# Attention scores as three 64-row products in alternating halves of the array, in a fused decoder block

## What is computed

```
q = xn @ Wq.T ; kv = xn @ Wkv.T ; k, v = kv[..., :64], kv[..., 64:]     # 16 heads of q, one k, one v
q, k = l2norm(q), l2norm(k)                                             # then both times sqrt(16)
sim = where(causal_mask, max_neg, einsum('bhid,bjd->bhij', q, k))
out = einsum('bhij,bjd->bhid', softmax(sim), v)
x = x + layernorm(out @ Wout.T, g2)
```

## Time and profile before

| | us |
|---|---|
| median of 3 runs (lowest, highest) | 1096.88 (1095.97, 1097.26) |
| the profiled execution, its time | 1095.58 |
| its span, first to last instruction | 1093.8 |
| TensorE busy (matmuls) | 917.9 |
| VectorE, ScalarE, GpSimd busy | 709.3, 444.0, 228.6 |

### The profile page before, as it was taken

One profiled execution on the slowest core, in us unless ns is written; L12 is line 12 of the kernel. 1 busy time (PEld: TensorE's weight loads), 2 busy tenths in 40 slices (PEclk: granted clock), 3 DMA queues, 4 the chain that ended last, 5 costly groups with the idle time before them and its releaser, 6 DMA issues.

```text
span 1093.8 us, 14277 instructions
## 1 busy us (share of the span) xinstructions
PE 917.9 (84%) x4446; PEld 676.6 (62%) x4446; DVE 709.3 (65%) x1607; ACT 444.0 (41%) x808; POOL 228.6 (21%) x282
## 2 busy tenths in 40 slices
PE   3698998898999987978989898999871089999997
PEld 2466666575766765755766566666551067777775
DVE  4466888868788877668787788877576322222221
ACT  1364643545454544434554445443342112222221
POOL 3232321211211123213122121201010611111111
PEclk8699998989998988989999999989985589999999
DMA  8300000000000000000000000000334500000000
GB/s 270 53 1 1 1 1 1 1 1 1 1 1 1 1 1 1 1 1 1 1 1 1 1 1 1 1 1 1 112 119 153 173 7 25 23 24 29 20 25 4
DMA packets 19176, 29.02 MB, mean 27 GB/s; under 512 B 2080, under 2 KB 15649, under 8 KB 19105
## 3 DMA queue, kind: packets, MB, share of 16 engines
q1 hardware_dynamic: 17008, 22.73, 7.0%
q0 software_dynamic: 1680, 4.21, 1.1%
q10 hardware_dynamic: 416, 1.18, 0.3%
HBM read 21.41 MB, written 7.10 MB: 26 GB/s over the span
## 4 chain that ended last, share of the span: by engine, by line
PE 36%; DVE 10%; issue 5%; POOL 3%; ACT 2%; DMA 1%; DVEq 0%; POOLq 0%; ACTq 0%
PE W L1278 6%; PE S L1255 5%; PE O L1255 5%; PE W L1166 2%; PE O L1095 2%; DVE ph L826 2%; PE O L1092 2%; PE W L1208 2%; PE S L1076 2%; PE S L1077 2%; PE O L1093 2%; POOL sorted_rows L581 2%; DVE junk L948 1%; DVE pl L828 1%; DVE mx L910 1%
## 5 line engine op out<-in xcount | busy, mean ns | idle before, releaser
L617 ACT ACTIVATE pr<-S 128x512 f32<-128x512 f32 x288 | 172.1, 598 | 255.5 <-PE S L1077 252.8
L828 DVE TENSOR_TENSOR pl<-pr,ph 128x512 fp32r<-128x512 f32 x288 | 206.0, 715 | 9.9
L1092 PE MATMUL O<-ph,vhi 128*65 128x512 f32 x288 | 145.6, 506 | 50.9 <-DVE ph L826 50.7
L826 DVE CAST ph<-pr 128x512 fp32r<-128x512 f32 x288 | 122.9, 427 | 54.5 <-POOL pr L535 38.6
L1095 PE MATMUL O<-pl,vhi 128*65 128x512 f32 x288 | 121.7, 423 | 1.7 <-DVE pl L828 0.5
L1076 PE MATMUL S<-qT,kT 128*128 128x512 f32 x288 | 120.1, 417 | 0.0
L1077 PE MATMUL S<-qT,kT 128*128 128x512 f32 x288 | 119.1, 414 | 0.0
L1093 PE MATMUL O<-ph,vlo 128*65 128x512 f32 x288 | 119.0, 413 | 0.0
L1092 PEld LDWEIGHTS O<-ph,vhi 128*65 128x65 f32 x288 | 41.5, 144 | 77.5 <-DVE ph L826 50.7
L528 POOL TENSOR_TENSOR rs<-ri,half 128x1 f32<-128x1 f32 x48 | 31.2, 650 | 238.0 <-DVE ri L762 238.0
L535 POOL TENSOR_SCALAR_AFFINE_SELECT pr<-pr 128x512 f32<-128x512 f32 x64 | 45.5, 711 | 166.3 <-ACT pr L617 166.3
(11 more groups left out here) (169 smaller groups left out, 1643.5 us busy)
## 6 DMA issues: line engine op xcount, KB each, us to landing
raw<-in_w_v SPq DMA_DIRECT2D x16, 512.0 KB, 6.3
wps<-in_w_proj SPq DMA_DIRECT2D x4, 1024.0 KB, 9.3
sorted_rows<-pad_row SPq DMA_DIRECT2D x19, 128.5 KB, 5.0
xs<-sorted_rows SPq DMA_DIRECT2D x19, 128.5 KB, 2.0
wqkv<-in_wqkv_t ACTq DMA_DIRECT2D x1, 1152.0 KB, 6.2
wout<-in_wout_t SPq DMA_DIRECT2D x1, 1024.0 KB, 10.0
xall<-in_x SPq DMA_DIRECT2D x1, 1024.0 KB, 11.0
xall<-in_x SPq DMA_DIRECT2D x1, 768.0 KB, 7.9
```

The source lines that it names most:

```text
L617: nc.scalar.activation(pr[:, k % RING, :], S[k % AHEAD][:], ACT.Exp, scale=SIM_SCALE)\
L826: nc.vector.tensor_copy(ph[:, k % RING, :], pr[:, k % RING, :]).then_inc(ph_ready, 1)
L828: nc.vector.tensor_tensor(pl[:, k % RING, :], pr[:, k % RING, :], ph[:, k % RING, :].bitcast(F32), ALU.subtract).then_inc(pl_ready, 1)
L1092: nc.tensor.matmul(o, vhi[:, vs, 0:DH + 1], ph[:, k % RING, :], start=j == 0, stop=False)
```

## The change

- **Scores.** The parts of q are no longer stacked. `qTh` and `qTl` hold high and low parts of two heads one under the other, 64 rows each. Of eight neighbouring heads the four even ones are now a group with an even number and use rows 0 to 63, the four odd ones are the next group and use rows 64 to 127. Per step there are three products of 64 rows (high by high, key high by q low, key low by q high), and the scores of two steps, (t, g, j) and (t, g + 1, j), are issued together, product by product, alternating between the halves and two banks. The fourth product, low by low, is left out.
- **Order.** Steps go (g, j), (g + 1, j), (g, j + 1) and so on, so O0 and O1 fill at the same time. Scores are issued every second step, for the steps four and five ahead; there are four banks S, two banks W. `LATER` is 3 for VectorE and 4 for ScalarE and GpSimd. Rings are 6 deep. A tile too short for side work gets 8 empty positions first, then its steps.
- **Exponential.** Off the diagonal ScalarE takes it twice from the bank: into `ph` in fp32r, then into `pr`; VectorE's cast stays on the diagonal alone.
- **Turning.** `qn` is turned in full float32, two heads at a time: eight transposes in two jobs, and one for the doubled key. ScalarE copies a job out as the high part, then VectorE subtracts that from the bank for the low part (`q_low`) and so frees the bank. `lows_early` sees that the subtraction stands, in the order, ahead of the job that needs its bank. GpSimd makes the value's parts itself (`v_parts`).
- **Hidden turn** of the feed-forward: banks S2, S3 in place of W2, S2.

The diff, cut to its core:

```diff
-RING = 4
+RING = 6
 KV = TPB + 2
 XS = 4
-WB = 3
+WB = 2
...
-    ("out_turn", 0, -1, 0.10), ("q_high", 0, 1, 0.11), ("out_turn", 1, -1, 0.12), ("q_low", 0, 1, 0.16),
+    ("out_turn", 0, -1, 0.10), ("k_double", 0, 1, 0.08), ("out_turn", 1, -1, 0.12), ("v_parts", 0, 1, 0.16),
...
-AHEAD = 3
-
-
-LATER = {"pe": 0, "dve": 2, "act": 3, "pool": 3}
+AHEAD = 4
+
+
+LATER = {"pe": 0, "dve": 3, "act": 4, "pool": 4}
...
     for t in range(TILES):
-        for g in range(GROUPS):
-            start.append(len(steps))
-            steps += [(t, g, j) for j in range(t % TPB + 1)]
+        start.append(len(steps))
+        for g in range(0, GROUPS, 2):
+            steps += [(t, g + s, j) for j in range(t % TPB + 1) for s in range(2)]
     start.append(len(steps))
     return steps, start
...
+def lows_early(here):
+
+    owed = []
+    for stages in here:
+        n = 0
+        while n < len(stages):
+            name, part, t = stages[n]
+            if name in READER:
+                for entry in owed:
+                    entry[1] += 1
+                for key, _ in [entry for entry in owed if entry[1] >= WB]:
+                    for later in here:
+                        if key in later:
+                            later.remove(key)
+                    n = stages.index((name, part, t))
+                    stages.insert(n, key)
+                    n += 1
+                owed = [entry for entry in owed if entry[1] < WB]
+                if name == "q_turn":
+                    owed.append([("q_low", part, t), 0])
+            elif name == "q_low":
+                owed = [entry for entry in owed if entry[0] != (name, part, t)]
+            n += 1
...
-            own = range(start[GROUPS * slot], start[GROUPS * (slot + 1)])
+            own = range(start[slot], start[slot + 1])
             ks = []
             most = len(own) - AHEAD
             for n, k in enumerate(own[:most]):
-                ks += [k] + [None] * (max(most, MIN_POSITIONS - AHEAD) * (n + 1) // most - len(ks) - 1)
-            ks += own[most:]
+                ks += [k] + [None] * (max(most, MIN_POSITIONS) * (n + 1) // most - len(ks) - 1)
+            if most <= 0:
+                ks = [None] * MIN_POSITIONS
+            ks += own[max(most, 0):]
...
-        HT = [W[2], S[2]]
+        HT = [S[2], S[3]]
...
-                    elif name == "q_low":
-
-                        pool.wait_ge(qhi_ready, t + 1)
-                        pool.wait_ge(qlo_ready, t + 1)
+                    elif name == "v_parts":
+
+                        pool.wait_ge(qn_ready, t + 1)
                         if t >= KV:
-                            pool.wait_ge(pv_done, group_start[GROUPS * TPB * ((t - KV) // TPB + 1)])
+                            pool.wait_ge(pv_done, tile_start[TPB * ((t - KV) // TPB + 1)])
                         vs = t % KV
-                        nc.gpsimd.tensor_copy(vhi[:, vs, 0:DH], qhl[:, HEADS + 1, 0, :].bitcast(F32)).then_inc(v_ready, 1)
-                        nc.gpsimd.tensor_copy(vlo[:, vs, 0:DH], qhl[:, HEADS + 1, 1, :].bitcast(F32)).then_inc(v_ready, 1)
+                        nc.gpsimd.tensor_copy(vhi[:, vs, 0:DH], qn[:, HEADS + 1, :]).then_inc(v_ready, 1)
+                        pool.wait_ge(v_ready, 2 * t + 1)
+                        nc.gpsimd.tensor_tensor(vlo[:, vs, 0:DH], qn[:, HEADS + 1, :], vhi[:, vs, 0:DH].bitcast(F32),
+                                                ALU.subtract).then_inc(v_ready, 1)
...
-                act.wait_ge(pv_done, group_start[G_ + 1])
+                act.wait_ge(pv_done, group_last[G_] + 1)
...
+                    if not on_diagonal(k):
+                        if k >= RING:
+                            act.wait_ge(pv_done, k - RING + 1)
+                        nc.scalar.activation(ph[:, k % RING, :], S[k % AHEAD][:], ACT.Exp, scale=SIM_SCALE)\
+                            .then_inc(ph_by_act, 1)
...
-                    elif name == "q_high":
-                        act.wait_ge(qn_ready, t + 1)
-                        if t >= 1:
-                            act.wait_ge(side_ready, job_count("q_turn", 4, t - 1))
-                            act.wait_ge(v_ready, 2 * t)
-                            act.wait_ge(kdup_ready, 2 * t)
-                        nc.scalar.copy(qhl[:, :, 0, :], qn[:]).then_inc(qhi_ready, 1)
-                    elif name == "q_turn" and part < 4:
+                    elif name == "q_turn" and part < 2:
                         act.wait_ge(side_ready, job + 1)
                         if t >= 2:
-                            act.wait_ge(s_ready, group_start[GROUPS * (t - 1)])
-                        nc.scalar.copy(qT[t % 2][:, 4 * part:4 * part + 4, :].rearrange("p h q -> p (h q)"),
-                                       W[job % WB][:]).then_inc(act_freed, 1)
-                    elif name == "q_turn" and part == 4:
+                            act.wait_ge(s_ready, tile_start[t - 1])
+                        nc.scalar.copy(qTh[t % 2][:, 4 * part:4 * part + 4, :].rearrange("p h q -> p (h q)"),
+                                       W[job % WB][:]).then_inc(qth_ready, 1)
+                    elif name == "q_turn" and part == 2:
                         act.wait_ge(side_ready, job + 1)
                         if t >= KV:
-                            act.wait_ge(s_ready, group_start[GROUPS * TPB * ((t - KV) // TPB + 1)])
-                        nc.scalar.copy(kT[:, t % KV].rearrange("p a k -> p (a k)"), W[job % WB][:, 0:2 * P])\
-                            .then_inc(act_freed, 1)
+                            act.wait_ge(s_ready, tile_start[TPB * ((t - KV) // TPB + 1)])
+                        nc.scalar.copy(kT[:, t % KV, 0, :], W[job % WB][:, 0:P]).then_inc(qth_ready, 1)
...
-                    nc.vector.tensor_copy(ph[:, k % RING, :], pr[:, k % RING, :]).then_inc(ph_ready, 1)
-                    dve.wait_ge(ph_ready, k + 1)
+                    if on_diagonal(k):
+                        nc.vector.tensor_copy(ph[:, k % RING, :], pr[:, k % RING, :]).then_inc(ph_by_dve, 1)
+                    ph_wait(dve, k)
...
+                    elif name == "k_double":
+                        dve.wait_ge(qn_ready, t + 1)
+                        nc.vector.tensor_copy(kdup[:], qn[:, HEADS, :].unsqueeze(1).broadcast_to([P, 2, DH])).then_inc(kdup_ready, 1)
                     elif name == "q_low":
-                        dve.wait_ge(qhi_ready, t + 1)
-                        nc.vector.tensor_tensor(qhl[:, :, 1, :], qn[:], qhl[:, :, 0, :].bitcast(F32), ALU.subtract)\
-                            .then_inc(qlo_ready, 1)
-                        dve.wait_ge(qlo_ready, t + 1)
-                        for n in range(2):
-                            nc.vector.tensor_copy(kdup[:, n], qhl[:, HEADS, n, :].bitcast(F32).unsqueeze(1).broadcast_to([P, 2, DH]))\
-                                .then_inc(kdup_ready, 1)
+                        turn = job_of["q_turn", part, t]
+                        dve.wait_ge(qth_ready, 3 * t + part + 1)
+                        if part < 2:
+                            nc.vector.tensor_tensor(
+                                qTl[t % 2][:, 4 * part:4 * part + 4, :].rearrange("p h q -> p (h q)"), W[turn % WB][:],
+                                qTh[t % 2][:, 4 * part:4 * part + 4, :].rearrange("p h q -> p (h q)").bitcast(F32),
+                                ALU.subtract).then_inc(dve_freed, 1)
+                        else:
+                            nc.vector.tensor_tensor(kT[:, t % KV, 1, :], W[turn % WB][:, 0:P],
+                                                    kT[:, t % KV, 0, :].bitcast(F32), ALU.subtract).then_inc(dve_freed, 1)
...
-                    pe.wait_ge(p_ready, k - AHEAD + 1)
+                    pe.wait_ge(p_ready, k - AHEAD + 2)
                 if g == 0 and j == 0:
 
-                    pe.wait_ge(act_freed, freed_count("q_turn", 4, t))
+                    pe.wait_ge(dve_freed, freed_count("q_turn", 2, t))
                 ks = (t - t % TPB + j) % KV
-                q = qT[t % 2][:, HPG * g:HPG * (g + 1), :].rearrange("p h q -> p (h q)")
-                nc.tensor.matmul(S[k % AHEAD][:], kT[:, ks, 0, :], q, start=True, stop=False)
-                nc.tensor.matmul(S[k % AHEAD][:], kT[:, ks, 1, :], q, start=False, stop=True).then_inc(s_ready, 1)
+                for n, (a, q) in enumerate(((0, qTh), (0, qTl), (1, qTh))):
+                    for half_ in range(2):
+                        rows = slice(DH * half_, DH * (half_ + 1))
+                        mm = nc.tensor.matmul(S[(k + half_) % AHEAD][:], kT[rows, ks, a, :],
+                                              q[t % 2][rows, 2 * g:2 * g + 4, :].rearrange("p h q -> p (h q)"),
+                                              start=n == 0, stop=n == 2)
+                        if n == 2:
+                            mm.then_inc(s_ready, 1)
...
-            for k, stages in program("pe"):
-                if k == 0:
-                    for n in range(AHEAD):
```

(17 more changed lines are left out.)

68 lines of the change are left out of this document (45 added, 23 removed).

## The result

| | us |
|---|---|
| before, median of 4 runs (lowest, highest) | 1096.43 (1095.66, 1097.26) |
| with the change, median of 4 runs (lowest, highest) | 1117.61 (1115.78, 1123.96) |
| ratio, 95% interval | 1.0203 (1.0162 to 1.0245) |

The kernel became 21 us slower; the forecast was 1063 us, 34 us faster. The time lies inside the stated range, on the other side of no change.

The account below looks back on a forecast made before the run. TensorE was taken as the bound, VectorE second. The terms -33.1 - 15.8 - 35 + 30 + 20 gave -34 us: 1061.7 us for a profiled execution, 1063 us for the median, in a range of 1015 to 1135.

Parts of the forecast that it names:

- Part 1, the scores: Score products on TensorE: two halves run side by side, 0.69 us a pair for 0.92, -33.1 us.
- The mode switch: Rival, chance 0.17: array drains between whole and half rows, 0.16 us at both ends of 144 pairs, +46, 1109 us.
- the "no overlap" rival: Rival, chance 0.12: the six half-row score products follow one another, 99 us over the forecast, 1162 us.
- The estimate from the packing figure: Score pairs: by the skill's 3.07 ratio a set costs 1.30 of one matmul; 30 of the 33 us gone again.
- Part 2, turns: Turning queries on TensorE: 144 fewer transposes at 0.11 us each, -15.8 us.
- Part 3, VectorE: Cast kept on the diagonal steps only, relieving TensorE's waits for VectorE: -35 us, between 0 and 75.
- Part 4, ScalarE at nothing: Second exponential on 224 steps adds 110 to 134 us to ScalarE, 37 us of other work gone; costed at nothing.
- Part 5, group ends: End of a pair of groups: TensorE waits 1.0 us for the copy of O at 31 places, +30 us (0 to +62).
- Part 6, side banks: Two side banks for three: 0.05 us for each of 426 side jobs, +20 us, between 0 and +64.
- the rival decides: Side-bank rival, chance 0.13: 0.15 us for 426 jobs, 1107 us; it decides from 0.13 us a job.
- Part 7, nothing: Value parts on GpSimd, deeper ring, hidden turn's new banks and DMAs: no cost.

Follow-up runs that it names:

- a_full4: The changed kernel with four 128-row score products a pair of steps in place of the six of 64 rows; 1095.18 us, ratio to before 0.9983.
- a_full3: The changed kernel with three 128-row score products a pair of steps in place of the six of 64 rows; 1083.78 us, ratio to before 0.987.
- b_half_rows: The kernel before with its two score products a step over rows 0 to 63 alone, without pairs or second exponential; 1231.22 us, ratio 1.1222.
- a_full4_late: The `a_full4` kernel with banks taken alternately and both steps reported ready with the last product; 1110.42 us, ratio to before 1.0119.
- a_cast: The changed kernel with VectorE's cast on every step and one exponential, as before the change; 1150.47 us, ratio to before 1.0477.

## Why the prediction was wrong

**Part 1, the scores: the step that failed.** The term was -33.1 us. Against `a_full4`, which has the old number of products in the new frame, the halves cost +22.4: 55.5 us apart, and the forecast missed by 54.6. Two things were wrong in it. The mode switch, which stood as a rival at 0.17, is real: 0.30 us a pair up to the first whole product, 0.36 in the mean with the one behind it, 52 us of TensorE's time, where the rival said 2 x 0.16 = 0.32 and 46.

The Trainium skill's sentence "Mode switching requires drain" ("TensorEngine Tiling (Array Packing)", Key Properties) agrees with these intervals; its rule told against the change and was given too little weight beside an argument that no row spoke for it, when no row could.

The second: TensorE's time was taken as the kernel's time. 33 us of products less (`a_full3` against `a_full4`) gave 11.4. That is the other 22 us; the first 34 are those between `a_full3` and the changed kernel. That the halves overlap fully was right (the "no overlap" rival is out). The estimate from the packing figure of the Trainium skill ("TensorE: Matmul & The Clock Gate", part 3), 1.3 times the length of one, did not come true: away from the switch a pair of half products takes the 0.23 us of one whole product. The shown lengths, 0.50 us for the two and 0.49 for one alone in `b_half_rows`, agree, though the ends of matmuls are modelled.

The switch rival's 1109 is within 9 us of the time, and part of that is luck. It was the forecast plus its price, and it kept the forecast's gain from a shorter score part, of which a third came. It left out that the pair also reports its scores late (`a_full4_late`, 15 us with a longer delay), which no part had costed, and it took 46 us as full time where the half rows' 52 us on TensorE cost 34.

**Part 2, turns**: -15.8; doubling them cost 12 to 14. About right, as far as that tells what leaving them out gives.

**Part 3, VectorE**: -35, measured -17 in the old order and -33 in the new one. The new wait of `pl` for the second `pr` was not in it, nor was the clock. **Part 4, ScalarE at nothing**: right in that it is no bound (`a_cast`).

**Part 5, group ends**: +30, measured +3 with one exponential ahead of the copy. What the copy's place costs with two was 8 us. The values of the odd group and a side job lie between; the prediction named this cover and priced it at none.

**Part 6, side banks**: +20, measured +36, and +45 beside two exponentials, 0.08 and 0.11 us a job; inside the stated 64 and under the 0.13 from which the rival decides.

**Part 7, nothing**: the stretch behind the attention stage, taken as left alone, took 5 us more; the cause stays open.

The parts other than the scores came to -0.8 us in the prediction and to -2.7 in `a_full4`. That is errors cancelling. With the measured prices (two exponentials and two banks +28.5, order +3, turns -13) one would expect +18; 21 us are then missing. Most of them may lie in the price of the second exponential: with the 33 us that it is worth in the new order in place of 17 the sum is about +2. The other candidates are four score banks and looking four steps ahead, which were not tried alone; a higher granted clock (0.97 in the stage of `a_full4`, 0.94 before) goes with any of these. Which it is stays open.

Of the range and chances: 1117.6 lies in 1015 to 1135 because the switch was in it. Slower had 0.32; with the Trainium skill's rule for it and no row against it, the switch's 0.17 was too low. That the time came out only 21 us over the kernel before owes something to a term that the prediction did not have, the clock.

## What to carry to other kernels

Before 64-row products are put among 128-row ones, count the places where the two kinds meet: here each way in and out cost 0.35 us or more, more than the overlap of three products saved (0.23). If later pairs of half products keep to 0.23 us, then at three pairs for four whole products a run of them would have to be five pairs or longer to pay on TensorE, an estimate that no run here tests. The busy share of the bound engine doesn't price a product taken from it: 33 us less of TensorE's products gave 11, and the rest came back as waits. Ask also when the first result of a batch is complete, not only how long the batch is. And where a change is made of several parts, try each alone: here one of them was worth 1.6% and was hidden under the others.

## What the runs showed of the hardware that was not expected

- Two products in different halves of the array take as long as one: away from a switch the next pair starts after 0.23 us. With the grouped order in the program the trace shows the same side-by-side pairs, and the time is the same (1117.7 and 1117.6 us). A product of the free half started ahead of earlier ones of the busy half, each pair within about 0.01 us.
- The change of rows shows in three intervals of 0.33 us where 0.23 is usual, two going in and one coming out, and in a fourth, behind the first whole product, that is 0.05 to 0.10 us too long. This is so whether one half is used or both. At the lower clock level the three are 0.56, 0.59 and 0.56 us where 0.43 is usual (`b_half_rows`). At both places the weight load starts with its product, and not 0.23 us ahead of it.
- With one half used and the other empty, at every step, the granted clock fell to 0.85 over the attention stage and once stood at its lower level for 48 us on end while TensorE was shown as busy throughout. With both halves used, at every second step, it was 0.97. What in the activity makes the difference these runs do not tell.
